# A recurrent cell on one core: error rows from transposed predictions, cell 1's h in one operation, the candidates' bias pass beside their products, and a later place for the entry's split

## The reference

```
encoded   = tanh(xt @ We + st @ Ue + be)                     # 24 wide
new_state = tanh(xt * Wx[c] + st * Ws[c] + bk[c])            # 8 candidates c, 32 wide each
mem       = [ (encoded, err) , mem[0..18] ]                  # the last 20 entries of 25 numbers
a         = relu(mem.flat @ enc_w1 + enc_b1)                 # 500 -> 64
agent_in  = relu(a @ enc_w2 + enc_b2)                        # 64 -> 16
h1, c1    = lstm(agent_in, h1, c1);  h2, c2 = lstm(h1, h2, c2)
gate      = softmax(h2 @ gate_w + gate_b)
theta     = clamp01(2.5 * mean(|last 10 errors|))
gate      = gate * theta + gate_before * (1 - theta)
st        = sum over c of gate[c] * new_state[c]
pred      = clamp01(st[-1]);  err = pred - yt
```

## Time and profile before

| | |
|---|---|
| time, median of 3 runs | 5462.91 us (5460.96 to 5463.51) |
| profiled execution, own time | 5460.57 us |
| its span | 5458.7 us |
| PE busy / PEld busy | 5391.8 us (99%) / 3426.0 us (63%) |
| DVE / ACT / POOL busy | 4479.8 (82%) / 3807.2 (70%) / 2421.7 us (44%) |
| TensorE's granted clock | 0.998 of full speed |
| items | 512 |

### The profile page before, as it was taken

One profiled execution on the slowest core, in us unless ns is written; L12 is line 12 of the kernel. 1 busy time (PEld: TensorE's weight loads), 2 busy tenths in 40 slices (PEclk: granted clock), 3 DMA queues, 4 the chain that ended last, 5 costly groups with the idle time before them and its releaser, 6 DMA issues.

```text
span 5458.7 us, 188210 instructions
## 1 busy us (share of the span) xinstructions
PE 5391.8 (99%) x67584; PEld 3426.0 (63%) x67584; DVE 4479.8 (82%) x12336; ACT 3807.2 (70%) x9729; POOL 2421.7 (44%) x4613
## 2 busy tenths in 40 slices
PE   8999999999999999999999999999999999999998
PEld 5666666666666666666666666666666666666665
DVE  7888888888888888888888888888888888888887
ACT  5777777777767777777777777777777777777775
POOL 3444444444444444444444444444444444444444
PEclk9999999999999999999999999999999999999999
DMA  2111111111111111111111111111111111111111
GB/s 69 29 29 32 29 32 29 32 29 32 29 32 29 32 29 30 31 29 32 29 32 29 32 29 32 29 32 29 30 31 29 32 29 32 29 32 29 32 29 40
DMA packets 299285, 172.38 MB, mean 32 GB/s; under 512 B 156734, under 2 KB 263882, under 8 KB 298714
## 3 DMA queue, kind: packets, MB, share of 16 engines
q1 hardware_dynamic: 293568, 159.42, 11.2%
q10 hardware_dynamic: 5146, 3.66, 0.2%
HBM read 74.65 MB, written 2.10 MB: 14 GB/s over the span
## 4 chain that ended last, share of the span: by engine, by line
PE 95%; DVE 4%; issue 1%; DMA 0%; POOL 0%; ACT 0%; DVEq 0%; ACTq 0%; POOLq 0%
PE a_ps L366 26%; PE chain L417 17%; PE cand_ps L338 9%; PE a_ps L377 9%; PE cand_ps L347 7%; PE chain L310 5%; PE chain L317 4%; PE chain L403 4%; PE chain L293 4%; PE a_ps L388 3%; PE chain L435 3%; PE cand_ps L330 3%; DVE mixed L799 1%; DVE state L817 1%; DVE added L720 1%
## 5 line engine op out<-in xcount | busy, mean ns | idle before, releaser
L366 PE MATMUL a_ps<-hist,w_hist 125*64 125x512 f16 x12288 | 1896.3, 383 | 24.1 <-DMA w_hist<-enc_table 24.1
L817 DVE TENSOR_REDUCE state<-mixed 128x64 f32<-128x512 f32 x2048 | 1353.4, 682 | 34.2 <-POOL mixed L920 0.8
L920 POOL TENSOR_TENSOR mixed<-cand,gate 128x512 f32<-128x512 f32 x1024 | 1281.1, 1272 | 48.6 <-POOL gate L908 12.5
L554 ACT ACTIVATE cand<-cand_ps 128x512 f32<-128x512 f32 x2048 | 1101.8, 593 | 91.1 <-PE cand_ps L347 90.6
L417 PE MATMUL chain<-cell_in,cell_w 128*64 128x128 f32 x16384 | 1120.7, 278 | 19.8 <-DVE cell_in L735 19.8
L886 POOL TENSOR_TENSOR one_theta<-ones,theta 128x8 f32<-128x8 f32 x512 | 103.4, 202 | 2241.0 <-DVE theta L702 2241.0
L417 PEld LDWEIGHTS chain<-cell_in,cell_w 128*64 128x64 f32 x16384 | 889.2, 136 | 271.5 <-DVE cell_in L735 211.8
L366 PEld LDWEIGHTS a_ps<-hist,w_hist 125*64 125x64 f16 x12288 | 681.4, 109 | 536.2 <-issue 141.7
L561 ACT ACTIVATE gates<-chain 128x384 f32<-128x384 f32 x1024 | 502.0, 490 | 726.3 <-PE chain L417 726.1
L735 DVE SCALAR_TENSOR_TENSOR cell_in<-gates,tanh_c 64x128 f32<-64x128 f32 x2048 | 582.5, 284 | 127.0 <-ACT tanh_c L571 113.4
L720 DVE SCALAR_TENSOR_TENSOR added<-gates 128x256 f32<-128x256 f32 x1024 | 537.1, 524 | 141.2 <-ACT gates L561 141.2
(11 more groups left out here) (76 smaller groups left out, 6823.8 us busy)
## 6 DMA issues: line engine op xcount, KB each, us to landing
x_sb<-in_x_l SPq DMA_DIRECT2D x260, 256.0 KB, 2.7
hist<-entry_parts SPq DMA_DIRECT2D x2048, 25.0 KB
w_hist<-enc_table SPq DMA_DIRECT2D x258, 128.0 KB, 2.4
y_rows<-in_y_l SPq DMA_DIRECT2D x260, 8.0 KB
ys<-in_y ACTq DMA_DIRECT2D x1, 2048.0 KB, 16.3
preds_out<-preds SPq DMA_DIRECT2D x1, 2048.0 KB, 7.5
cand<-in_encoder ACTq DMA_DIRECT2D x1, 640.0 KB, 3.8
cell_w<-in_cell ACTq DMA_DIRECT2D x2, 256.0 KB, 4.5
```

Source lines behind the costliest of these rows:

```text
L366: nc.tensor.matmul(a_ps[g][ENC * half:ENC * half + ENC, :], w_hist[0:HROWS, w_slot(u), kk, wp, :], hist[0:HROWS, xp, k, at:at + 512], star ...
L554: ins = nc.scalar.activation(cand[:, g, q // 2, :, q % 2, :, :].rearrange("p h s c -> p h (s c)"), cand_ps[q][:, :].rearrange("p (h k) -> ...
L817: V.tensor_reduce(state[:, g, hf, 2 * pair:2 * pair + 2, :], mixed[:, pair, hf, :, :, :], AX, ALU.add)\
L920: G.tensor_tensor(mixed[:, 0, :, q, :, :], cand[:, g, 0, :, q, :, :], over_s, ALU.mult)\
```

## The change

- `prediction_transpose`: two new transposes on TensorE turn `pred_now` (already clipped) into four rows of `cand_ps[0]`; `errors` subtracts `y_rows` from them. `at_least_zero` and its buffer go. The second half of `w_we` and `w_ue` is widened from 36 to 64 columns, and the column that copied the state's last row goes.
- Cell 1's h is made by one operation of 128 partitions into `h_second` in place of two of 64. `gate_logits` reads it with two matmul calls of 64 columns in place of four of 32. `keep_hidden` (two ScalarE copies) brings it to `cell_in[1]` for the next step.
- `candidates_bias` moves from ahead of `cell_gates(cur, 0)` to behind it. The pairs of `history` are spread anew, and `history_waits(new)` stands behind `bias_of_cell(cur, 0)` with all of `history(new, 0)` after it.
- ScalarE: `entry_high` moves behind `encoder1`, `agent_input` ahead of `next_hidden`. VectorE: `prediction` right behind the sums, `totals` and `reciprocals` from the end of a phase to the start of the next.
- GpSimd: `entry_low` is done for `cur` and not for `new`, behind both `mix_quarter`s, and waits for `q_h[0]` of the same item. SP's own order is unchanged.

The diff, cut to its core (`first_hidden` is the old `new_hidden` for cell 0, and `prediction`, `new_error` and `keep_prediction` only get another order of the eight values of `pred_now`):

```diff
-ENTRY_ROWS = (slice(0, HALF), slice(HALF, ER))
+ENTRY_ROWS = (slice(0, HALF), slice(HALF, P))
...
-        gate_w = sb("gate_w", [P, HF, Q * C])
+        gate_w = sb("gate_w", [P, TILES * C])
...
+        h_second = sb("h_second", [P, GROUPS, P])
...
+            def prediction_transpose(item):
+                g, n, u = item
+                pe.wait_ge(q_pred, n)
+                pe.wait_ge(q_cand[0], n)
+                for hf in range(HF):
+                    last = nc.tensor.matmul(cand_ps[0][0:Q, P * hf:P * hf + P],
+                                            pred_now[:, g, Q * hf:Q * hf + Q], ident[:, :], is_transpose=True, start=True, stop=True,
+                                            skip_group_check=True)
+                last.then_inc(q_predps, 1)
...
                 if c == 0:
                     pe.wait_ge(q_enc, n)
-                    pe.wait_ge(q_rl, n)
+                    pe.wait_ge(q_err, n)
...
                     pe.wait_ge(q_hnext, n)
                 else:
+                    pe.wait_ge(q_hkept, n)
                     pe.wait_ge(q_h[0], n)
...
                 pe.wait_ge(q_h[1], n)
-                for hf in range(HF):
-                    for rows in CELL0_OUT:
-                        last = nc.tensor.matmul(chain[g][rows, 0:TILES * C]
-                                                .rearrange("p (a h k) -> p a h k", a=2, h=HF)[:, :, hf, :],
-                                                cell_in[1][:, g, hf, rows], gate_w[:, hf, :],
-                                                start=False, stop=True, skip_group_check=True)
+                for rows in CELL0_OUT:
+                    last = nc.tensor.matmul(chain[g][rows, 0:TILES * C], h_second[:, g, rows], gate_w[:, :],
+                                            start=False, stop=True, skip_group_check=True)
...
                 if cur:
-                    history(cur, 2, 0, 1)
                     state_transpose(cur, 0)
                     state_transpose(cur, 1)
+                    history(cur, 2, 0, 1)
+                    prediction_transpose(cur)
+                    encoded_s(cur)
                     history(cur, 2, 1, 3)
                     history(cur, 3, 0, 1)
-                    encoded_s(cur)
-                if new:
-                    history_waits(new, extra)
-                    history(new, 0, 0, 1)
-                if cur:
-                    history(cur, 3, 1, 2)
                 if old:
                     logit_bias(old)
-                if new:
-                    history(new, 0, 1, 2)
-                if old:
                     gate_logits(old)
                 if cur:
-                    history(cur, 3, 2, 3)
+                    history(cur, 3, 1, 3)
                     encoder1_now(cur)
                     bias_of_cell(cur, 0)
                 if new:
-                    history(new, 0, 2, 3)
+                    history_waits(new, extra)
+                    history(new, 0)
+                if cur:
+                    encoder2(cur)
+                if new:
                     history(new, 1, 0, 2)
                 if cur:
-                    encoder2(cur)
+                    cell_gates(cur, 0)
                     candidates_bias(cur)
-                if new:
-                    history(new, 1, 2, 3)
-                if cur:
-                    cell_gates(cur, 0)
                     candidates_x(cur)
                     candidates_s(cur)
...
                     cell_gates(cur, 1)
+                if new:
+                    history(new, 1, 2, 3)
...
-            def at_least_zero(item):
-                g, n, u = item
-                act.wait_ge(q_zps, n)
-                nc.scalar.activation(clamped[ZR:ER, g, :], chain[g][ZR:ER, Z_AT:Z_AT + COLS], ACT.Relu)\
-                    .then_inc(q_rl, 1)
...
+            def keep_hidden(item):
+                g, n, u = item
+                act.wait_ge(q_h[1], n)
+                for hf in range(HF):
+                    rows = CELL1_OUT[hf]
+                    last = nc.scalar.activation(cell_in[1][rows, g, hf, :], h_second[rows, g, :], ACT.Copy)
+                last.then_inc(q_hkept, 1)
...
                 if new:
-                    at_least_zero(new)
                     encoded(new)
-                    entry_high(new)
                 if cur:
                     candidates(cur, 2)
                     exponentials(cur)
                 if new:
                     encoder1(new)
-                if cur:
+                    entry_high(new)
+                    agent_input(new, 0)
+                if cur:
+                    keep_hidden(cur)
                     next_hidden(cur, 0)
                 if new:
-                    agent_input(new, 0)
                     cell_tanhs(new, 0)
...
             def errors(item):
                 g, n, u = item
-                dve.wait_ge(q_rl, n)
-                V.scalar_tensor_tensor(entry[ZR:ER, g, :], clamped[ZR:ER, g, :], 1.0,
-                                       y_rows[ZR:ER, x_slot(u), g, :], ALU.min, ALU.subtract)\
+                dve.wait_ge(q_predps, n)
+                V.tensor_tensor(entry[ZR:ER, g, :], cand_ps[0][0:Q, 0:COLS], y_rows[0:Q, x_slot(u), g, :],
+                                ALU.subtract)\
                     .then_inc(q_err, 1)
...
+            def second_hidden(item):
+                g, n, u = item
+                dve.wait_ge(q_tanhc[1], n)
+                dve.wait_ge(q_out_gate[1], n)
+                V.scalar_tensor_tensor(h_second[:, g, :], gates[1][:, g, 0, :], 1.0, tanh_c[1][:, g, :],
+                                       ALU.add, ALU.mult).then_inc(q_h[1], 1)
...
                 if old:
+                    totals(old)
+                    reciprocals(old)
                     fresh_gate(old)
                     new_gate(old)
...
                     mix_sum(old, 1, 0)
                     mix_sum(old, 1, 1)
+                    prediction(old)
                 if cur:
                     error_sum(cur)
                     cell_terms(cur, 1)
...
                     cell_value(cur, 1)
-                    thetas(cur)
-                if old:
-                    prediction(old)
-                if cur:
-                    new_hidden(cur, 1, 0)
-                    new_hidden(cur, 1, 1)
                 if new:
                     errors(new)
                 if cur:
+                    second_hidden(cur)
+                    thetas(cur)
                     peaks(cur)
                     below_peak(cur)
-                    totals(cur)
-                    reciprocals(cur)
...
             def entry_low(item):
                 g, n, u = item
                 pool.wait_ge(q_eh, n)
+                pool.wait_ge(q_h[0], n)
                 G.tensor_tensor(entry_parts[:, g, 1, :], entry[:, g, :], entry_parts[:, g, 0, :],
                                 ALU.subtract).then_inc(q_el, 1)
...
                     mix_quarter(old, 0)
                 if cur:
-                    kept_share(cur)
-                    kept_gate(cur)
+                    entry_low(cur)
                 if old:
                     new_error(old, extra)
                     keep_prediction(old, extra)
-                if new:
-                    entry_low(new)
-                if cur:
+                if cur:
+                    kept_share(cur)
+                    kept_gate(cur)
                     weighted_exponentials(cur)
```

More of the change, by code:

```diff
@@ L501, in _ @@
             load(w_enc2[:, :], w["enc2"])
-            load(gate_w[:, :, :].rearrange("p h c -> p (h c)"), w["gate_w"])
+            load(gate_w[:, :], w["gate_w"])
             load(indicator[:, :], ind_c)
@@ L677, in _ @@
                 link(V.tensor_scalar(some, some, scale, None, ALU.mult))
-            link(V.tensor_scalar(gate_w[:, :, :], gate_w[:, :, :], 0.5, None, ALU.mult))
+            link(V.tensor_scalar(gate_w[:, :], gate_w[:, :], 0.5, None, ALU.mult))
             dve.wait_ge(s_hist0, 1)
@@ L683, in _ @@
             dve.wait_ge(s_y[0], 16)
-            first = y_rows[ZR:ER, 0, :, :].rearrange("p g b -> p (g b)")
+            first = y_rows[0:Q, 0, :, :].rearrange("p g b -> p (g b)")
             link(V.tensor_scalar(first, first, -1.0, None, ALU.mult))
@@ L727, in cell_value, with first_hidden @@
                                        added[c][:, g, 0, :], ALU.mult, ALU.add).then_inc(q_cell[c], 1)
-            def new_hidden(item, c, hf):
+            def first_hidden(item, hf):
                 g, n, u = item
-                rows = (CELL0_OUT, CELL1_OUT)[c][hf]
-                if hf == FIRST_HALF[c]:
-                    dve.wait_ge(q_tanhc[c], n)
-                    dve.wait_ge(q_out_gate[c], n)
-                last = V.scalar_tensor_tensor(cell_in[1][rows, g, hf, :], gates[c][rows, g, 0, :], 1.0,
-                                              tanh_c[c][rows, g, :], ALU.add, ALU.mult)
-                if hf != FIRST_HALF[c]:
-                    last.then_inc(q_h[c], 1)
```

(27 more changed lines are left out.)

33 lines of the change are left out of this document (15 added, 18 removed).

## The result

The changed kernel takes 5804.6 us (5804.49 to 5804.91, 4 runs) against 5461.93 us (5460.07 to 5463.51) before: 1.063 times as long, 95% interval 1.061 to 1.064. The forecast was 5660 us, with a range of 5560 to 5755 us. The direction and the mechanism held; the size was too small, 199 us forecast and 343 us measured.

What follows compares the result with a forecast made beforehand. The entry's ring (10.91 us), longer than TensorE's own queue (10.84), was to set the phase: 0.39 us over 10.52, times 510 phases, +199 us on 5460.57, so 5660 us, range 5560 to 5755.

Steps and rivals of the forecast that it cites:

- The ring: From S through cell 0's h, GpSimd's split, SP's four DMA issues and the landing, back to S: 10.91 us (10.84 to 11.3).
- the waits: TensorE at `history`'s first product waits for the DMA of `hist`, about 500 times, 0.05 to 0.3 us each.
- S: The point in TensorE's phase at which `history(new, 0)` starts; the forecast counted 11.01 us from it to the next, less 0.10.
- TensorE's own queue: TensorE's phase summed over six places, a to f: 10.84 us (10.73 to 11.09), against 10.52 before.
- a: One pair of `history`, then up to the state's transposes: 0.25 us in place of 0.32, gain 0.07 (bounds 0 and 0.10).
- b: State's transposes to `encoded_s`: stays 1.06 us, the two new transposes hidden where two pairs moved away; uncovered, up to 0.46.
- c: `encoded_s`, pairs, logits, `encoder1_now`, cell 0's bias: one pair more (+0.22), logits 0.10 less, so 2.89 us against 2.77.
- d: To encoder 2 and on to cell 0's products: no gain, 1.71 us, since the activation's latency is what is paid.
- e: Cell 0's products to cell 1's: candidates' bias (0.35) comes in, wait for h goes; 4.00 us against 3.73, +0.27.
- f: Cell 1's products on TensorE: unchanged at 0.93 us.
- The first rival: The landing is in time and TensorE's queue alone sets the phase: 10.84 us, +163 us, 5624 us; chance 0.25.
- the 0.59 us of `cell_terms`: VectorE operation meeting GpSimd's mixing: full lock would give 0.73 us, the row 0.59, read as half that delay; alone 0.42.

## Why the prediction was right and wrong

**Right.** The ring from `history_waits` over h, split, SP and the landing sets the phase; it was shown from four sides: taken away by the old place (5424.6 us), shortened by a second issuer (5443.1), lengthened by an issue (6169) and by an earlier wait in the queue (7561). The split starts 0.14 us after h, the waits are where they were announced, and the clock stayed at 0.998.

**Wrong, the ring's sizes.** This is the step that failed. 10.91 us was too short by 0.28 for the turn shown. Three terms were too small: the 0.10 us from the last data to TensorE measured 0.30, three pairs and the step to encoder 2 measured 0.77 and not 0.66, and GpSimd needed 0.14 and not 0.08 to start; against them `cell_terms` was wholly free of the mixing, 0.08 to the good. The 0.11 us more at encoder 2 is no wait for `a_sb`, which was ready at 3010.87, ahead of S. The trace of before showed when data moved, not when TensorE may go on; my 0.10 was taken from compute engines. The Trainium skill (DMA: Bandwidth & Descriptors, Why a DMA increments its semaphore by 16 and not by 1) says that each DMA engine's increment of the semaphore lands only after that engine's data. The trace agrees: the last data are there by 3021.80, the DMA counts as landed at 3022.06, and TensorE starts 0.04 us later. The average phase, 11.24 us, is 0.05 longer than this turn, since every other one takes 11.25 to 11.34. That rest is SP's too. The four issues of the turn before the one shown (it took 11.24 us) and of the turn shown are these:

```profile
3005.81 3.69 SPq L271 DMA_DIRECT2D hist<-entry_parts  x4
...
3017.05 3.63 SPq L271 DMA_DIRECT2D hist<-entry_parts  x4
```

Averaged over 300 phases of the trace, the issuing takes 0.08 us more and starts 0.02 us later in the longer ones, and all other links are the same. 510 times the 0.33 us between 10.91 and 11.24 is 168 us, which covers the 145 us missed; the rest stems from the reference phase, for 0.39 us was counted from 10.52 and the average before is 10.56.

**Wrong, TensorE's own queue.** It was to be 10.84 us and is 10.49, a gain. These are the same six places in the kernel with the split in its old place, with mine in brackets: a 0.32 (0.25), b 1.02 (1.06), c 2.82 (2.89), d 1.69 (1.71), e 3.78 (4.00), f 0.87 (0.93). Its timeline, from which a, e, f and the second part of d are read:

```profile
3005.07 0.43 PE L398 MATMUL a_ps<-a_sb,w_enc 128*32 128x128 f32 x8
...
3006.00 1.09 PE L428 MATMUL chain<-cell_in,cell_w 128*64 128x128 f32 x16
3007.03 0.39 PE L340 MATMUL cand_ps<-cand_bias,ones 32*128 32x512 f16 x4
...
3007.26 1.03 PE L348 MATMUL cand_ps<-w_x,x_sb 32*128 32x256 f32 x16
...
3009.53 1.28 DVE L830 TENSOR_REDUCE state<-mixed 128x64 f32<-128x512 f32 x2
...
3009.78 1.04 PE L428 MATMUL chain<-cell_in,cell_w 128*64 128x128 f32 x16
...
3010.65 0.39 PE L376 MATMUL a_ps<-hist,w_hist 125*64 125x512 f16 x2
...
3010.97 0.44 PE L293 MATMUL chain<-ident,state 128*128 128x128 f32 x2
```

The failing term is e. I charged the candidates' bias 0.35 us, its cost ahead of the products and with a pair beside it, and left the next block as it was; it takes 0.23 us here and makes the next block 0.1 us shorter. As this queue was not what ended last, the error did not move the forecast, and that was luck: it would have, had the split stayed. The first rival, "TensorE's queue alone", would have been 5425 and not 5624 us, on the other side of no change. The transposes did hide, as said in b. A small reading in a was wrong as well: I took its 0.32 us in the kernel before for a wait for VectorE's sums. Here the sums end at 3010.81, 0.16 us before the transposes start, and a still takes 0.32, so one pair of 0.22 us and some 0.10 us of step to the fp32 transposes fill it; three pairs and the step to encoder 2 show the same tenth. What TensorE does in it was not traced.

**Wrong, a reading.** I took the 0.59 us of `cell_terms` for half of a delay. VectorE's operation ended 0.28 us after GpSimd's mixing (3014.87 after 3014.59), 0.29 us after it in the long phase (3004.34 after 3001.55 + 2.50), and 0.28 us after the split without the wait (3005.59 after 3005.31). The mixing of that long phase in the kernel before:

```profile
3001.55 2.50 POOL L920 TENSOR_TENSOR mixed<-cand,gate 128x512 f32<-128x512 f32 x2 [0.24 <-POOL gate L908]
```

All 510 meetings of the two in the trace of before end so, 0.28 us after the mixing, though they last from 0.55 to 1.15 us. So the operation is held until GpSimd's ends and then needs 0.28 of its 0.42 us. That bears out the full lock of the Trainium skill (SBUF — State Buffer, Who interferes with whom), which I had weighed as half wrong.

## What to carry to other kernels

Before work is moved later in its phase, follow its result round to the instruction that will wait for it and write down the whole ring, with the DMA issues one by one and what lies between the last data and the waiting engine; a slack of 3 us can hide behind "it is needed only next phase" and be less than what the move takes. A filler block is not priced by its own length but by the stretch in which it stands: the same four matmuls cost 0.32 us in one place and 0.1 in the other. And a change of many parts is best judged part by part: here one part lost 380 us and the others together won some 35; the best version is the change without the late split, 5424.6 us, 0.9937 of before.

## What the runs showed of the hardware

- Between the last data of a DMA within SBUF and the start of the waiting matmul lay 0.30 us, all but 0.04 of it ahead of the landing as the trace counts it.
- TensorE's clock fell to half in some, not all, of the waits of about 3 us that stood once in each phase (0.894 over the run), while waits of 0.7 us in 11.2 left it at 0.998.
- A VectorE operation with two inputs in SBUF that met a GpSimd operation ended 0.28 us after it, with overlaps of 0.27 to 0.87 us.
- The loop's back edge left VectorE idle for 0.40 us a turn between `reciprocals` and `fresh_gate`:

```profile
DVE fresh L781 <- DVE recip L775: 20.0, 51, 0.5
```

The phase with it took 11.03 us in place of 10.52, since GpSimd's mixing was pushed onto `cell_terms`. Moving the two operations behind the back edge won 17 us, 0.33 us a turn.
